# A part of the first search's counting moves from the vector engine to the scalar engine, and v's low part and the lengths' guard move from GpSimd to the vector engine

## What is computed

```python
def top_k_block(emb_s, emb_t, attention_weights, k):        # attention_weights is x
    adj = emb_s * emb_t
    att = jax.nn.softmax(attention_weights, axis=-1) * (1.0 / np.sqrt(n))
    adj = (adj * att).at[:, diag, diag].set(-jnp.inf)
    _, idx = jax.lax.top_k(adj.reshape(g, n * n), k)          # k = 10240 of n*n = 1048576
    return jnp.zeros((g, n * n)).at[rows, idx].set(1.0).reshape(g, n, n)

def attention_block(x, emb, W_emb, b_emb, g_norm, W_qkv, g_q, g_k, W_out):
    scale, shift = jnp.split(emb @ W_emb + b_emb, 2, axis=-1)
    xn = _rms_norm(x, g_norm) * (1.0 + scale) + shift
    q, k, v = ...                                             # of xn @ W_qkv, 16 heads of 64
    q, k = _rms_norm(q, g_q), _rms_norm(k, g_k)
    attn = jax.nn.softmax(jnp.einsum('bhqd,bhkd->bhqk', q, k) * d ** (-0.5), axis=-1)
    o = jnp.einsum('bhqk,bhkd->bhqd', attn, v)                # back to (b, n, dim)
    return o + o @ W_out
```

## Time and profile before

| what | value |
|---|---|
| time before, median of 3 runs | 3856.68 us (3854.23 to 3859.69) |
| the profiled execution, its own time | 3864.25 us |
| span of its instructions | 3862.5 us |
| busy: PE, DVE, ACT, POOL | 93%, 63%, 50%, 68% |
| granted TensorE clock, mean share | 0.966 |

### The profile page before, as it was taken

How to read it: one execution, slowest core, us unless ns; L and a number is a source line. 1 busy time by engine, 2 the same in 40 slices (tenths; PEclk the granted TensorE clock), 3 DMA queues, 4 the chain that set the end, 5 groups by cost and what they waited for, 6 DMA issues and landing times.

```text
span 3862.5 us, 48132 instructions
## 1 busy us (share of the span) xinstructions
PE 3576.9 (93%) x16947; PEld 2587.2 (67%) x16963; DVE 2430.1 (63%) x3619; ACT 1950.5 (50%) x3269; POOL 2624.0 (68%) x3063
## 2 busy tenths in 40 slices
PE   4884899999999999999999999999999999999999
PEld 1324677777755677777755677777755677777754
DVE  8997666667678577777778577777777222222221
ACT  1005565655553555555554455555553455555550
POOL 2006788888865687887765678887865587878750
PEclk9996899999999999999999999999999999999999
DMA  7005222222336322222236322222235322222122
GB/s 284 0 0 169 91 101 99 99 99 99 101 122 215 109 88 83 87 88 82 84 125 215 105 82 88 88 88 82 82 126 167 111 88 88 82 82 95 70 83 91
DMA packets 163304, 399.50 MB, mean 103 GB/s; under 512 B 11848, under 2 KB 83584, under 8 KB 153216
## 3 DMA queue, kind: packets, MB, share of 16 engines
q1 hardware_dynamic: 163072, 396.52, 29.2%
HBM read 302.10 MB, written 94.37 MB: 103 GB/s over the span
## 4 chain that ended last, share of the span: by engine, by line
PE 38%; POOL 36%; DVE 13%; issue 6%; ACT 3%; DMA 3%; SPq 1%; POOLq 0%; DVEq 0%; ACTq 0%
POOL pl L519 13%; PE pax L1389 9%; PE pst L1362 7%; PE ppv L1462 6%; PE pst L1445 6%; POOL rs L609 5%; PE pax L1425 5%; POOL qkn L612 3%; DVE xr L1009 3%; PE ppv L1468 3%; DVE mx L1149 3%; POOL qkn L614 2%; POOL stage L626 2%; POOL stage L627 2%; POOL vl L630 2%
## 5 line engine op out<-in xcount | busy, mean ns | idle before, releaser
L519 POOL TENSOR_TENSOR pl<-pf,ph 128x1024 fp32r<-128x1024 f32 x512 | 1220.9, 2394 | 223.7 <-ACT pf L842 222.9
L982 DVE TENSOR_SCALAR_CACHE_REDUCE trash<-keys,state 128x2048 uint8<-128x2048 f32 x384 | 899.9, 2344 | 9.9
L1149 DVE TENSOR_REDUCE mx<-pax 128x1 f32<-128x512 f32 x960 | 618.2, 686 | 360.6 <-PE pax L1425 359.8
L836 ACT ACTIVATE ph<-pst 128x1024 fp32r<-128x1024 f32 x512 | 523.1, 1022 | 255.3 <-PE pst L1445 254.7
L1143 DVE TENSOR_REDUCE ss<-sq 128x4 f32<-128x256 f32 x256 | 107.3, 419 | 683.8 <-ACT sq L808 659.8
L842 ACT ACTIVATE pf<-pst 128x1024 f32<-128x1024 f32 x512 | 522.3, 1020 | 1.3 <-DMA out_x<-pf 1.3
L1389 PE MATMUL pax<-wh,xh 128*128 128x384 f32 x1920 | 392.0, 347 | 8.9 <-DVE mx L1149 4.7
L1425 PE MATMUL pax<-sA 65*128 65x512 f32 x960 | 361.0, 445 | 30.0 <-DVE mx L1149 13.9
L1389 PE MATMUL pax<-wl,xh 128*128 128x384 f32 x1920 | 384.1, 339 | 0.0
L1468 PE MATMUL ppv<-pl,vh 128*65 128x512 f32 x1024 | 366.6, 404 | 9.4 <-POOL pl L519 9.0
L1389 PEld LDWEIGHTS pax<-wh,xh 128*128 128x128 f32 x1920 | 338.0, 191 | 40.8 <-ACT vh L812 14.6
(11 more groups left out here) (174 smaller groups left out, 5728.2 us busy)
## 6 DMA issues: line engine op xcount, KB each, us to landing
xl<-xl_scr SPq DMA_DIRECT2D x224, 512.0 KB, 3.6
wh<-w_scr SPq DMA_DIRECT2D x24, 1536.0 KB, 6.3
wl<-w_scr SPq DMA_DIRECT2D x24, 1536.0 KB, 9.7
keys<-in_x SPq DMA_DIRECT2D x32, 512.0 KB, 5.6
xl_scr<-xlo SPq DMA_DIRECT2D x64, 256.0 KB, 3.6
wo<-wo_scr SPq DMA_DIRECT2D x4, 4096.0 KB, 14.4
pf<-out_x SPq DMA_DIRECT2D x64, 256.0 KB, 3.8
out_x<-pf SPq DMA_DIRECT2D x64, 256.0 KB, 3.1
```

Of the source, the lines that this page charges most:

```text
L519: e.tensor_tensor(pl[:, w % 3, :], pf[:, w % 3, :], ph[:, w % 3, :].bitcast(F32), ALU.subtract).then_inc(t_lo, 1)
L836: e.activation(ph[:, w % 3, :], src, ACT.Exp, scale=DH ** -0.5).then_inc(t_eh, 1)
L982: e.tensor_scalar(trash[:], kv, thr_f, None, ALU.is_ge, ALU.add, accum_out=cnt[:, c:c + 1]).then_inc(z_cnt, 1)
L1149: e.tensor_reduce(mx2[:, j // T, j % T, c:c + 1], max_banks(alone, j)[:, c, :], axis=AX, op=ALU.max).then_inc(m_mx, 1)
```

## The change

The first search is written out without a loop. In steps 1 to 31 DVE compares only the first 4608 of the 8192 keys, in three pieces. ACT compares the other 3584 (`SHARE`): one activation with Sign(threshold - key) into the rest of `mask`, whose sum per partition goes to `cnt[:, 0]`, and PE adds that sum with one more matmul, against `allp`. The mask is now "below the threshold" and `ones` holds 2.0, so that both parts count in the same scale. `reach` is no longer kept in the steps. After step 31 a last pass (`search_last`) forms the next float above the threshold, compares all 8192 keys with it and gives `reach`. PE runs 8 filling matmuls in a step, not 12, and the conditioning is spread over steps 16 to 31, two products in a step.

In the pairs DVE makes `ss / 64 + eps` itself and gives `a_ms`, on which POOL's power now waits. DVE also makes v's low part, straight from the PSUM bank (`value_low`), and it is this instruction that now gives `a_v`. ACT writes `vh` first and copies only q and k to `qkn`. In the boundaries v's low part stays on POOL (`alone=True`); the guard is on DVE there too.

```diff
-    UNROLL = 8
-    WARM = 12
+    WARM = 8
+    SHARE = 7 * (N // 2)
...
+    whole_cuts = [0, 3072, 5632, 7168, T * N]
+    part_cuts = [0, 2048, 3584, T * N - SHARE]
...
         def prep_scale(self, gp, t):
-            wait_apart(e, a_ss, u + 1, passed)
-            e.tensor_scalar(rs[:, cols], ss[:, cols], 1.0 / DH, EPS, ALU.mult, ALU.add).then_inc(a_rs, 1)
-            e.wait_ge(a_rs, 4 * u + 1)
+            wait_apart(e, a_ms, u + 1, passed)
             e.tensor_tensor(rs[:, cols], rs[:, cols], half4[:], ALU.pow).then_inc(a_rs, 1)
...
         def prep_parts(self, gp, t, par, alone=True):
+            if alone:
                 e.wait_ge(a_v, u + 1)
                 e.tensor_tensor(vl[:, par, t, :, 0:DH], v, vh[:, par, t, :, 0:DH].bitcast(F32),
                                 ALU.subtract).then_inc(a_vs, 1)
...
         def search_alone(self, b):                                     # Scalar
+            for z in range(1, STEPS):
+                e.wait_ge(y_up, 7 * z)
+                e.activation(mask[:, T * N - SHARE:], kv[:, T * N - SHARE:], ACT.Sign, scale=-1.0, bias=thr_f,
+                             accum_out=cnt[:, 0:1]).then_inc(y_act, 1)
...
         def prep_tile(self, gp, par, t, alone=False, z=None):          # Scalar
+            if not alone:
+                e.activation(vh[:, par, t, :, 0:DH], vp, ACT.Copy)
             wait(e, a_lo, u - 1)
+            if alone:
+                ...
+            else:
+                e.activation(qp[:, 0:4 * DH], bank[:, 0:4 * DH], ACT.Copy).then_inc(a_qk, 1)
...
         def search_alone(self, b):                                     # Vector
-            with e.Fori(0, STEPS // UNROLL) as q:
+            for z in range(STEPS):
...
+                wait(e, y_act, z)
                 e.tensor_copy(state[:], ahead[:, 0, :])
...
-                    wait_apart(e, y_up, n + 6, passed)
-                    e.copy_predicated(reach[:], acc[:], tot[:])
+                e.wait_ge(y_up, n + 6)
+                e.copy_predicated(state[:], acc[:].broadcast_to([P, 3]), ahead[:, 1, :]).then_inc(y_up, 1)
+                e.wait_ge(y_up, n + 7)
+            self.search_last(kv)
...
         def prep_sums(self, gp, t):
             e.wait_ge(a_sq, u + 1)
+            e.tensor_reduce(ss[:, cols], sq[:], axis=AX, op=ALU.add).then_inc(a_ss, 1)
+            wait(e, a_rs, 3 * u - 4)
+            e.wait_ge(a_ss, u + 1)
+            e.tensor_scalar(rs[:, cols], ss[:, cols], 1.0 / DH, EPS, ALU.mult, ALU.add).then_inc(a_ms, 1)
+
+        def value_low(self, gp, par, t):
+            e.wait_ge(a_qk, u + 1)
+            v = pax[:, 0, 4 * DH:6 * DH].rearrange("p (h d) -> p h d", h=2)
+            e.tensor_tensor(vl[:, par, t, :, 0:DH], v, vh[:, par, t, :, 0:DH].bitcast(F32),
+                            ALU.subtract).then_inc(a_v, 1)
...
         def search_alone(self, b):                                     # Tensor
+                if not alone:
+                    e.wait_ge(y_act, z)
+                    i = e.matmul(pst[:, 0, 0:1], allp[:], cnt[:, 0:1], start=False, stop=True, skip_group_check=True)
```

More of the change, by code:

```diff
@@ L1047, in ranks @@
             e.wait_ge(f_dve, n + 6)
-            e.scalar_tensor_tensor(r0[:], pre[:], neq[:], reach[:], ALU.subtract, ALU.add).then_inc(f_dve, 1)
+            ties = neq
+            if b == 0:
+                e.copy_predicated(carry[:], acc[:], neq[:]).then_inc(y_up, 1)
+                e.wait_ge(y_up, 7 * STEPS + 12)
+                ties = carry
+            e.scalar_tensor_tensor(r0[:], pre[:], ties[:], reach[:], ALU.subtract, ALU.add).then_inc(f_dve, 1)
             e.wait_ge(f_dve, n + 7)
@@ L1219, in search_alone @@
             e.wait_ge(c_pool, 7)
-            cuts = mask_cuts[1:]
-            def sums(z):
-                for j in range(T * N // HALF):
+            e.wait_ge(c_par, 1)
+            for z in range(STEPS + 1):
+                alone, cuts = z in (0, STEPS), cuts_of(z)[1:]
+                for j in range(cuts[-1] // HALF):
                     c = sum(j * HALF >= cut for cut in cuts)
-                    e.wait_ge(y_mask, len(cuts) * z + c + 1)
-                    i = e.matmul(pst[:, 0, :], ones[:, 0:P], mask[:, j * HALF:(j + 1) * HALF],
-                                 start=(j == 0), stop=(j == T * N // HALF - 1))
-                i.then_inc(y_sum, 1)
-            with e.Fori(0, STEPS // UNROLL - 1) as q:
-                for r in range(UNROLL):
-                    sums(UNROLL * q + r)
+                    e.wait_ge(y_mask, masks_before(z) + c + 1)
+                    i = e.matmul(pst[:, 0, :], ones[:, 0:P], mask[:, j * HALF:(j + 1) * HALF], start=(j == 0),
+                                 stop=(alone and j == cuts[-1] // HALF - 1), skip_group_check=True)
+                if not alone:
+                    e.wait_ge(y_act, z)
+                    i = e.matmul(pst[:, 0, 0:1], allp[:], cnt[:, 0:1], start=False, stop=True, skip_group_check=True)
+                i.then_inc(y_sum, 1)
+                if z == STEPS // 2:
+                    e.wait_ge(d_wemb, 16)
+                if STEPS // 2 <= z < STEPS:
+                    self.conditioning((z - STEPS // 2) // 2, z % 2)
+                else:
                     for _ in range(WARM):
                         e.matmul(pst[:, 1, :], ones[:, 0:P], ones, start=True, stop=True)
-            e.wait_ge(d_wemb, 16)
-            for k in range(KT):
-                sums(STEPS - KT + k)
-                self.conditioning(k)
             e.wait_ge(c_rows, 1)
@@ L1243, in search_alone, with conditioning @@
             i.then_inc(c_cnd, 1)
-        def conditioning(self, k):
+        def conditioning(self, k, half):
             e = self.e
             ct = paramsT[:, 0:NC].rearrange("p (b k) -> p k b", k=KT)
-            for c in range(4):
+            for c in range(2 * half, 2 * half + 2):
                 to = pst[0:B, 2 + c, :] if c < 2 else ppv[0:B, c - 2, :]
@@ L1252, in conditioning @@
                              start=(k == 0), stop=(k == KT - 1))
-            if k == KT - 1:
+            if k == KT - 1 and half:
                 i.then_inc(c_cnd, 1)
```

140 lines of the change are left out of this document (91 added, 49 removed).

## The result

The changed kernel takes 3765.23 us (median of 4 runs, 3762.16 to 3770.67), the kernel before 3856.65 us (median of 4, 3854.23 to 3859.69). The ratio is 0.9764, with a 95% interval from 0.9747 to 0.9781: the change makes the kernel 91 us faster. The prediction said 3774 us, with a range from 3745 to 3803. The profiled execution of the changed kernel has a span of 3763.9 us; before it was 3862.5.

The account below looks back on a forecast made before the run. It took DVE to bound the first search, and PE and POOL side by side the pairs. Search -57 and pairs -26 from the profiled 3864.25 gave 3781, or 3774 us at the runs' 0.2% lower median; range 3745 to 3803.

Parts of the forecast that it names:

- DVE's path: First search: with 4608 of 8192 keys compared on DVE, DVE could start the reduction at 3.6 to 3.75 us.
- Step 1: First search: ACT 4.4 us late, but DVE's shortened comparisons should be through before POOL begins; counted as 1 us lost.
- The term at tile 7: Pairs: PE's wait for `stage` falls from 2.14 to some 0.6 us, as POOL's work arrives 1.5 us earlier.
- +0.75 at tile 2: Pairs, batches 0 to 2: PE waits 0.75 us longer for the bank, DVE's subtraction standing behind the search update.
- +0.4: Pairs, tile 1: PE waits 0.4 us longer for the bank, DVE's subtraction coming behind ACT's shortened copy.
- -1.1 each: The 7 pairs of batch 3, which has no search: each 1.1 us shorter, -8 us together.
- The clock's 9 us: Pairs: a shorter wait at tile 7 keeps PE's clock up; 9 us gained, taken from 0 to 21.
- (a): Rival, chance 0.17: the search gains 57 us, the pairs only 3 because of new bank waits for PE; 3797 us.
- (b): Rival, chance 0.12: the search step is 5.5 us, from costlier Sign or DVE and ACT slowing each other; 3788 us.
- (c): Rival, chance 0.06: the pairs give nearly all of the wait and clock, and the search step is 4.8 us; 3745 us.
- (d): Rival, chance 0.04: PE's clock falls in the search, a step takes some 8.5 us; slower, 3881 us.
- (e): Rival, chance 0.03: counts on DVE hold up the next tile's sums, 0.7 us in each of 147 tiles; 3874 us.

Follow-up runs that it names:

- the filled kernel: The kernel before, with nine matmuls that nobody reads in front of the transposes of tile 7: 3845.34 us against 3855.45.

## Why the prediction came out right

**The search, -57 predicted, -60 in the trace, -62 measured alone.** The reduction at 3.9 us came at 3.84. "From there to the next step" I had taken as 1.15; it is 1.12. The step is 4.96 and not 5.05, which over 31 steps is the 3 us. The bound on ACT's path was right, since 4096 keys moved the reduction by just what Sign takes longer. DVE's path was put at 3.6 to 3.75; with this cut it stays under ACT's, but with 3072 keys on ACT it is PE's queue that sets 4.17. The last pass was mis-sized: 9 predicted, 10.1 measured. The missing term is PE's clock, which falls because PE has no work during the ten small instructions; filled, the pass takes 8.6 us. Step 1 was the other way about what I argued: DVE's comparisons were not through before POOL began and took 4.98 us, but ACT's lateness lay under that, and of the 1 us nothing shows.

**The pairs, -26 predicted, -30 measured alone.** The term at tile 7, from 2.14 to 0.6, came out at 0.71. The +0.75 at tile 2 was 0.75. Two were too low: "+0.4" at tile 1 was +0.76, since the guard is held there by POOL, and tile 4, counted as nothing, has 0.26 in some pairs. Against them stands a gain that I did not count, PE's wait for `pl` behind tile 7: in pairs where the clock stays up it fell from 0.79 to 0.37 us. So the sum per pair of batch 1 is -0.43 to -0.44 where I had -0.35, partly by errors that cancel. The pairs of batch 3 had "-1.1 each"; the undisturbed one there went from 90.0 to 88.6. The clock's 9 us are of the size of the 10 that the filled kernel gives, but they were a choice between 0 and 21, so that this fits is in part luck. The boundaries were sized too small, with 2 us in all. In the profile of the kernel with only the pairs changed, against that of before, the first pair begins 1.6 us earlier, and the three stretches from the last pair of a batch to the next batch are together 6.8 us shorter; what gives this was not taken apart. In the same two traces the 21 pairs of batches 0 to 2 are together 6.6 us shorter (7 predicted) and the 7 pairs of batch 3 18.5 us (8 and a part of the clock's 9).

**The rivals.** (a), that the pairs give nothing, fell with the kernel that has only their change. (b) fell with the step of 4.96, and (c) with it, since (c) wanted 4.8 and the pairs' whole wait. (d) did not come; the kernel without the filling matmuls shows that they are what keeps it away. (e) fell: the counts never held up the sums of squares, though they hold up a sum of the search at tile 2 where a held guard stands ahead of them (0.61 and 1.12 us in two of the experiments).

What the prediction did not see is that it added both moves as if each were needed. It said "POOL loses the guard and v's low part" and checked that POOL's tile got below PE's. It did not ask how little would do, and v's low part alone would have.

## What to carry to other kernels

Lateness that adds up over tiles is removed by a small relief on the late engine (here 0.43 us of a tile of 7.03); after that, a further task only burdens its new engine, so try each move alone. When work moves to DVE, look at what stands behind it on DVE: here the order of two instructions of 0.2 and 0.3 us decided more than 20 us. And when a step gets shorter, see what keeps PE busy in it: matmuls that nobody reads saved 25 us here, by one run.

## What the runs showed of the hardware

DVE's `tensor_scalar` on 128x4 elements between SBUF operands (the guard) takes 0.17 us. When it meets POOL's instruction on `pl` it lasts until that one ends: 0.55 and 0.56 us in the rows above, and 0.50 to 0.98 in four tiles of the pair from the kernel with v's low part on POOL, in which 132 of 256 guards are held. The same holds for a copy of two elements in step 1 beside POOL's L523: 2.25 us and not 0.16. DVE's subtraction with one operand in PSUM took 0.28 to 0.30 everywhere, beside POOL's work or not.

Sign on 3584 keys with a bias from memory takes 3.28 us, on 3072 keys 2.86 and on 4096 keys 3.71, so 0.83 ns for each further key; the prediction had 0.80.

The granted clock fell behind a pause of 2.9 us in the last pass. In the search without filling, with a pause of 2.5 us in every step, it stayed at 1.2 GHz from 80 to 110 us, which makes the step itself 1.78 us longer. With pauses of 0.75 us it stayed at 1.00. A pause of this length does not bring it down each time: before the change PE waits 2.27 us at tile 7 in the third and fourth pair of batch 1 as well, and both pairs run at full clock throughout. What else it takes, no run here shows.
